# Attention: the fourth bank of maxima of every eighth unit goes to ScalarE and GpSimd

## The reference

```python
dot = jnp.einsum('bqhs,bkhs->bhqk', queries, keys)
attn = jax.nn.softmax(dot, axis=-1)
out = jnp.einsum('bhqk,bkhs->bqhs', attn, values).reshape(b, t, e)
```

## Time and profile before

| what | us |
|---|---|
| median of 3 runs | 3694.74 (3690.15 to 3697.23) |
| the profiled execution's own time | 3692.36 |
| its span, from the first to the last instruction | 3690.5 |
| PE busy in the span (matmuls) | 3583.7 |
| DVE busy | 3200.7 |
| ACT busy | 2644.3 |
| POOL busy | 364.4 |

### The profile page before, as it was taken

One profiled execution on the slowest core, in us unless ns is written; L12 is line 12 of the kernel. 1 busy time (PEld: TensorE's weight loads), 2 busy tenths in 40 slices (PEclk: granted clock), 3 DMA queues, 4 the chain that ended last, 5 costly groups with the idle time before them and its releaser, 6 DMA issues. The chain is left out here.

```text
span 3690.5 us, 77992 instructions
## 1 busy us (share of the span) xinstructions
PE 3583.7 (97%) x31350; PEld 2038.0 (55%) x31350; DVE 3200.7 (87%) x4509; ACT 2644.3 (72%) x4958; POOL 364.4 (10%) x329
## 2 busy tenths in 40 slices
PE   6899999999999999999999999999998989999998
PEld 4577444444444444444444444444445678888887
DVE  7566899999999999999999999999966767766664
ACT  3455788989889998989998888999896432223332
POOL 0133100000000000000000000000002204303323
PEclk9899999999999999999999999999998999999999
DMA  6900321122021122113112203110012000132332
GB/s 187 226 24 18 108 33 18 10 23 30 4 30 26 7 23 22 18 10 36 18 10 23 30 3 30 26 7 7 4 45 70 35 2 31 54 104 56 82 86 39
DMA packets 297388, 149.13 MB, mean 40 GB/s; under 512 B 216097, under 2 KB 275559, under 8 KB 294480
## 3 DMA queue, kind: packets, MB, share of 16 engines
q1 hardware_dynamic: 284752, 133.61, 19.5%
q0 software_dynamic: 12288, 10.70, 1.7%
HBM read 86.44 MB, written 63.83 MB: 41 GB/s over the span
## 5 line engine op out<-in xcount | busy, mean ns | idle before, releaser
L1258 ACT ACTIVATE probs<-attention_scores_t_sums 128x512 f32<-128x512 f32 x4096 | 2142.4, 597 | 243.1 <-PE attention_scores_t_sums L1183 240.3
L1183 PE MATMUL attention_scores_t_sums<-q_operand,k_operand 50*128 50x512 f32 x2048 | 703.2, 443 | 8.0 <-ACTq L1273 6.2
L1177 PE MATMUL attention_scores_q_sums<-attention_k_operand,attention_q_operand 48*128 48x512 f32 x2048 | 699.8, 439 | 0.0
L1183 PE MATMUL attention_scores_t_sums<-attention_q_operand,attention_k_operand 50*128 50x512 f32 x2048 | 698.9, 443 | 0.0
L1177 PE MATMUL attention_scores_q_sums<-k_operand,q_operand 48*128 48x512 f32 x1952 | 670.2, 440 | 0.2
L1295 DVE TENSOR_REDUCE max_parts<-attention_scores_q_sums 128x1 f32<-128x512 f32 x1008 | 641.9, 676 | 1.1 <-PE attention_scores_q_sums L1177 1.1
L1295 DVE TENSOR_REDUCE attention_max_parts<-attention_scores_q_sums 128x1 f32<-128x512 f32 x992 | 631.9, 676 | 0.0
L1288 DVE TENSOR_REDUCE max_parts<-attention_scores_q_sums 128x2 f32<-128x1024 f32 x504 | 608.6, 1208 | 4.8 <-PE attention_scores_q_sums L1177 4.7
L1193 PE MATMUL attention_o_psum_sums<-probs,v_heads 128*32 128x256 f32 x8192 | 602.2, 389 | 0.0
L1193 PE MATMUL attention_o_psum_sums<-probs,attention_v_heads 128*32 128x256 f32 x8192 | 600.6, 388 | 0.0
L1288 DVE TENSOR_REDUCE attention_max_parts<-attention_scores_q_sums 128x2 f32<-128x1024 f32 x496 | 599.8, 1209 | 0.4 <-PE attention_scores_q_sums L1177 0.4
(11 more groups left out here) (335 smaller groups left out, 4621.2 us busy)
## 6 DMA issues: line engine op xcount, KB each, us to landing
expert_rows<-attention_empty_rows SPq DMA_DIRECT2D x16, 516.0 KB, 5.7
v_scratch<-value_chunk SPq DMA_DIRECT2D x16, 512.0 KB, 5.0
w_whole<-in_L_ffn_ew SPq DMA_DIRECT2D x8, 1024.0 KB, 6.8
experts_w_whole<-in_L_ffn_ew SPq DMA_DIRECT2D x8, 1024.0 KB, 5.7
q_operand<-q_scratch SPq DMA_DIRECT2D x24, 256.0 KB, 4.7
k_operand<-k_scratch SPq DMA_DIRECT2D x24, 256.0 KB, 6.4
attention_q_operand<-q_scratch SPq DMA_DIRECT2D x24, 256.0 KB, 4.9
attention_k_operand<-k_scratch SPq DMA_DIRECT2D x24, 256.0 KB, 6.6
```

Of the source, the lines that this page charges most:

```text
L1177: nc.tensor.matmul(SA[:, (2 * h + j) * CH:(2 * h + j + 1) * CH], QOP[b][64 * h:64 * h + ROWS, qt * P:(qt + 1) * P], KOP[b][64 * h:64 * h + ...
L1183: nc.tensor.matmul(ST[bank_n][:, :], KOP[b][64 * h:64 * h + ROWS + 2, kt * P:(kt + 1) * P], QOP[b][64 * h:64 * h + ROWS + 2, c * CH:(c + 1 ...
L1258: nc.scalar.activation(PR[:, tile, :], ST[bank_n][:, :], ACT.Exp).then_inc(st_free, 1)
```

## The change

In every eighth unit (`s % 8 == 3`: s = 27, 35 and so on, which are multiplied in loop units 3 and 11), DVE leaves out the reduce of the fourth bank. ACT copies that bank, 512 scores for each of 128 queries, from PSUM to memory on the chip (`COPY`), behind the fourth exponential of the loop unit. POOL folds the copy: the upper half is compared with the lower by a subtraction, a maximum with 0 and an addition, on 256, 128, ... and 1 columns, and the last addition writes the part that DVE would have written. POOL's operations depend on each other, and each waits for the one before. PE waits for the copy before it writes the fourth bank of the next unit; ACT waits, before it copies, for the fold of eight units earlier; DVE's maximum over the parts waits for the round's folds, by `msplit`, which now counts four a round (two folds, two splits) in place of two.

```diff
+        COPY, OVER = sb("scores_copy", [P, CH]), sb("scores_excess", [P, CH // 2])
...
+        def given(s):
+            return s >= LEAD and s % 8 == 3
...
-                sp.wait_ge(msplit, 2 * n + 2)
+                sp.wait_ge(msplit, 4 * n + 1)
...
+            step = Chain(pool, tail.chain, NCH * 3)
+            def fold(s, par):
+                pool.wait_ge(a_copied, copies(s))
+                w = CH // 2
+                while w:
+                    first, second, over = COPY[:, 0:w], COPY[:, w:2 * w], OVER[:, 0:w]
+                    step(nc.gpsimd.tensor_tensor(over, second, first, ALU.subtract))
+                    step(nc.gpsimd.tensor_scalar(over, over, 0.0, None, ALU.max))
+                    if w > 1:
+                        step(nc.gpsimd.tensor_tensor(first, first, over, ALU.add))
+                    w //= 2
+                u = s % U
+                nc.gpsimd.tensor_tensor(MPART[par][:, 1, u // 4, 2 * (u % 4) + 1:2 * (u % 4) + 2], COPY[:, 0:1], OVER[:, 0:1],
+                                        ALU.add).then_inc(msplit, 1)
             def split_max(n, par):
+                for s in (n * U + 3, n * U + 11):
+                    if given(s):
+                        fold(s, par)
                 pool.wait_ge(neg_ready, n + 1)
...
                 pe.wait_ge(sa_free, 4 * s + 2 * h + j + 1)
+                if h and j and given(s - 1):
+                    pe.wait_ge(a_copied, copies(s - 1))
...
+            def copy_scores(s):
+                if given(s - 8):
+                    act.wait_ge(msplit, folds(s - 8))
+                act.wait_ge(sa_ready, 4 * s + 4)
+                nc.scalar.copy(COPY[:, :], SA[:, 3 * CH:4 * CH]).then_inc(a_copied, 1)
...
                                 exps((u + 1) % 4 * 4 + t, count(i, r, u, t), bank(r, u, t))
+                            if t == 3 and given(g * U + u + LEAD) and not (last and r + (u + LEAD) // U >= HALF):
+                                copy_scores(g * U + u + LEAD)
...
-                for j in range(2):
+                for j in range(1 if given(s) else 2):
                     dve.wait_ge(sa_ready, 4 * s + j + 3)
...
-                                            AX.X, ALU.max).then_inc(sa_free, 1)
+                                            AX.X, ALU.max).then_inc(sa_free, 2 if given(s) else 1)
...
-                dve.wait_ge(msplit, 2 * splits)
+                dve.wait_ge(msplit, 4 * splits - 1)
```

More of the change, by code:

```diff
@@ L1025, in attention_phase @@
         max_out = sem("neg_max_written")
+        a_copied = sem("scores_q_copied")
         mrow_loaded = [sem(f"neg_max_row_loaded{b}") for b in range(2)]
@@ L1041, in count, with copies, folds @@
             return FIRST + i * TILES + r * ROUND + 4 * u + t
+        def given(s):
+            return s >= LEAD and s % 8 == 3
+        def copies(s):
+            return (s - LEAD - 3) // 8 + 1
+        def folds(s):
+            return 4 * (s // U) - 2 + (s % U) // 8
         def halves(body):
@@ L1152, in split_max @@
                 nc.gpsimd.tensor_tensor(MS[par][:, :, 0, :], NEG[:, :, :], ZERO[:, :, :], ALU.add).then_inc(msplit, 1)
-                pool.wait_ge(msplit, 2 * n + 1)
+                pool.wait_ge(msplit, 4 * n)
                 nc.gpsimd.tensor_tensor(MS[par][:, :, 1, :], NEG[:, :, :], MS[par][:, :, 0, :].bitcast(F32),
```

## The result

The changed kernel takes 3770.85 us (median of 4 runs, 3767.78 to 3772.16) against 3692.44 for the kernel before on the same chip: a ratio of 1.0206, 95% interval 1.0193 to 1.0218. It is slower by about 77 us. The forecast was slower by 55 (51 to 64), in a range of 3713 to 3800.

What follows compares the result with a forecast made beforehand. DVE was taken as full, with a PE-ACT loop nearly as long; the copy makes DVE 0.44 us late at 125 chosen units, 55 us (51 to 64) on 3692.4, so 3747, or 3749 as median; range 3713 to 3800.

Steps and rivals of the forecast that it cites:

- What bounds the kernel: Attention: DVE has no gaps, but PE and ACT form a second loop, 4.57 us for two units against DVE's 4.66.
- The lead of PE over DVE: At unit 5's first scores PE is 0.08 us ahead of DVE; before unit 4's first reduce, 0.22 us.
- The copy: On ACT ahead of unit 4's four exps: delays them 0.52 us (0.49 to 0.59), making DVE 0.44 us late.
- The two stops: Behind each chosen unit DVE idles for PE twice, about 0.38 and 0.66 us.
- The fold: On GpSimd, 27 dependent operations take 8.5 to 12.0 us; 10.3 taken, just fitting the 10.4 before DVE's maximum.
- the nine operations on one tensor: In the fold, without a row of their own: 0.9 to 4.4 us, 2.7 if like those with two tensors.
- the fold is late: DVE's maximum waits for the fold once a round, 63 times: 50 us more at 11.2 us, giving 3799; chance 0.24.
- a sign of being wrong: DVE idle for POOL ahead of its maximum over the parts would show the fold's length as the failed term.
- PE's added wait: PE waits for the copy ahead of the matmul of unit 4's fourth bank; claimed to cost nothing.
- ACT's wait for the fold of eight units earlier: On ACT before a copy: costs nothing unless a fold takes 18.78 us.
- The faster rival: ACT's idle 0.27 + 0.21 us in two units takes the copy in: 62 us go, 3632; chance 0.09.
- the third rival: DVE wins back its 0.44 us in six units, leaving 3 us more, 3697; chance 0.14.

Runs made afterwards that it cites:

- the skip alone: Against the changed kernel, the chosen units' fourth bank is left out altogether, nothing copied or folded, POOL adds two zeros: 3686.26 us, ratio 0.9973.
- the cut in every unit: Against the kernel before, DVE's reduce of the fourth bank is cut to 8 of 512 columns in every unit, no copy, no fold: 3666.05 us, ratio 0.9922.
- both kernels that gain: Changed kernel with the fourth bank left out, nothing copied or folded (3686.26 us), and changed kernel with loop units 2 and 10 chosen (3685.4 us).
- the three kernels with nothing else: Changed kernel without DVE's skip and with one POOL operation for the fold (3738.81 us), with loop units 1 and 9 (3738.43), with three operations fewer per fold (3735.26).
- units 1 and 9: Changed kernel with s % 8 == 1 chosen in place of s % 8 == 3, nothing left out: 3738.43 us, ratio 1.0113.
- one operation more: Changed kernel with one more small dependent operation (0.28 us) at the end of each fold, its result unused: 3787.21 us, ratio 1.0254.

## Why the prediction was right, and where it was off

**What bounds the kernel.** Right. That DVE's stage has a second loop of PE and ACT nearly as long as DVE's own, shown by the skip alone (10 us of 75) and the cut in every unit (29 of 400). The lead of PE over DVE that was read from the rows, 0.08 us, is the gain that is left: 0.09 to 0.10 measured in both kernels that gain. The reading of 18.78 us for eight units was of the longer kind of round; most have 18.68.

**The copy.** Right in place and kind, a little large. It was put at 0.52 us, between 0.49 and 0.59; it is 0.47, below the lower end: the copy of 0.58 us begins 0.11 before the exp ahead of it ends, and the next exp 0.11 before the copy's end. Behind the late tile's load PE's product came 1725.22 - 1724.79 = 0.43 us later, not 0.48 as in the earlier trace rows; the tile's matmul now begins with its load, where in the kernel before it began 0.16 us behind it (1716.20). So DVE loses 0.35 us at a chosen unit, not 0.44, and 125 x 0.35 = 44 us, not 55; the three kernels with nothing else have 42. The two stops came as forecast, 0.37 and 0.57 us for 0.38 and 0.66. DVE's busy time fell by 47 us and not by 75. An estimate gives the rest: DVE now stops 313 times (250 for PE, 63 for POOL), and at each stop 0.08 us that two neighbours shared count for one alone, 25 us in all.

**The fold.** This is the step that failed: "I take 10.3, ... that just fits". It takes 10.89 and doesn't. The terms for two-tensor operations (5.5 us forecast; 5.56 by the changed kernel's forms, summed) and for the gaps (2.1; 2.17 as the remainder) were right; the nine operations on one tensor were mis-sized, taken to cost what the two-tensor ones do, 2.7 us, and measured at 3.15. They lie inside the bounds of 0.9 to 4.4, and the half microsecond between 10.4 and 10.9 is by how much the fold is late. The rival "the fold is late" held, with 0.48 us of waiting in place of 0.8. Its full price is a little more than the wait: with the restart of DVE the first reduce of unit 8 and the next one's are 3.02 us apart, where a round in time has 2.33 + 0.13 = 2.46 (the maximum's pitch is 0.13 before, from 1726.13 to the row below, and 1735.44 - 1735.30 = 0.14 here), so 0.56, and 63 x 0.56 = 35 us. 44 + 35 = 79 against 77 measured.

```profile
1726.26 1.27 DVE L1295 TENSOR_REDUCE max_parts<-attention_scores_q_sums 128x1 f32<-128x512 f32 x2
```

**The number and the luck in it.** The case that the forecast took as the likeliest, a dear copy and a fold in time, did not come about; the rival with a chance of 0.24 did. DVE idle for POOL ahead of its maximum was named beforehand as a sign of being wrong, and it is there. The time lies inside the range because the range had that rival in it, and near enough to the 55 us because two misses went against each other: the copy was put 11 us too dear, and the 35 us of the late fold were not in the sum.

**What else was costed at nothing** held: PE's added wait (no row of its own), ACT's wait for the fold of eight units earlier (no row either), POOL's work beside DVE's reduces. The rounds went from 37.4 or 37.6 us to about 38.65; the forecast, with the fold in time, was 38.4, and with the copy behind odd units and the fold in time, or no fold, most rounds take 38.1.

**The faster rival** fell with the skip alone: 10 us, where the skip with a hidden copy was to give 62. Relieving DVE is worth some 29 us at the most while PE and ACT stay as they are, since the run that took 400 us from it left it waiting for PE. By the rule of the Trainium skill's page Perfetto Trace Analysis (section Identifying the Most-Contended Engine) DVE was the engine to relieve. The trace agreed on its occupancy, and the runs show that its occupancy was not what set the time.

The delay being made good by DVE's slack, the third rival, was not seen: the copy's cost stayed in all kernels that have it in odd units. That PE could be let go further ahead, by another order of its matmuls, was not tried.

## What to carry to other kernels

An engine without a gap may be only just the slowest of two loops; before moving work off it, read at the moved instruction how far its feeder is ahead, because that lead, and not the work moved, is the gain. Work moved to an engine with idle time costs nothing only at the places in its order where it idles: the same copy cost 42 us behind an odd unit's exps and nothing behind an even one's. A long chain of small operations is costed by each kind that is in it and compared with its due time, and where the sum lands within its error of the due time, choose an earlier unit: with units 1 and 9 the 35 us of the late fold were gone.

## What the runs showed that was not expected

- A wait of PE of 1.49 us once a round, in a stage where it is otherwise busy, was followed in 57 rounds of 62 by a granted clock of 0.50 for some microseconds, and in five by none below 1.00; over two stretches of 1200 us the clock was 0.94 and 0.93 in place of 1.00, and the kernel lost 160 us beyond the wait itself. What sets the five rounds apart is not shown. Waits of 0.4 us (the changed kernel) and 0.7 us (one operation more) left it at 1.00:

```profile
PE attention_scores_q_sums L1214 <- DVE max_parts L1341: 21.3, 31, 0.7
```

- On POOL a maximum of one tensor with a constant is slower than a subtraction or an addition of two tensors: 849 against 733 to 737 ns on 256 columns, (849 - 233) / 248 = 2.5 ns a column against (737 - 203) / 248 = 2.2.
